# Graph attention layer: the index list copied first in a group, two operands in PSUM, the next scores between the adds

## The reference

```
s_u = x @ W_u.T + b_u                # 8 heads
s_v = x @ W_v.T
e = s_u[src] + s_v[dst]
e = jnp.where(e >= 0, e, 0.2 * e)
m = segment_max(e, dst)
e_exp = jnp.exp(e - m[dst])
denom = segment_sum(e_exp, dst)
msg = xh[src] * (e_exp / denom[dst])[:, None, :]
out = segment_sum(msg, dst)
x = layernorm(x + out)
```

## Time and profile before

| what | value |
|---|---|
| median of 3 runs | 4935.61 us (4934.03 to 4941.12) |
| profiled execution, its own time | 4929.81 us |
| its span | 4928.1 us |
| PE busy | 3099.3 us, 63% |
| VectorE busy | 2202.6 us, 45% |
| GpSimd busy | 3434.9 us, 70% |
| ScalarE busy | 908.4 us, 18% |
| gathers of layer 1 (L1466), 880 | 1008.1 us busy, 605.6 us idle before them |

### The profile page before, as it was taken

The page is one execution under the profiler, slowest core; times in us unless marked ns, Lnnn a source line. Parts: engine busy times, 40 slices in busy tenths (PEclk is TensorE's granted clock), DMA queues, the critical chain, the costliest instruction groups (busy, mean ns, idle before and its releaser), DMA issues. The chain is left out here.

```text
span 4928.1 us, 61408 instructions
## 1 busy us (share of the span) xinstructions
PE 3099.3 (63%) x13554; PEld 1900.6 (39%) x13555; DVE 2202.6 (45%) x5019; ACT 908.4 (18%) x2810; POOL 3434.9 (70%) x2948
## 2 busy tenths in 40 slices
PE   3547877777777777877778768834444444444441
PEld 1224444444444444444444435523333333333331
DVE  2543333333333333333333349855555555555554
ACT  0212222222222222222222223300000000000002
POOL 4238888888888888888888867756666666666564
PEclk9869898888998888888898889956666666666665
DMA  7777767667767677677677666643333333333332
GB/s 285 193 241 137 135 126 136 133 123 135 132 126 138 127 131 134 126 135 132 123 136 132 123 133 206 181 148 93 95 92 100 93 94 91 96 98 94 92 93 66
DMA packets 471760, 641.52 MB, mean 130 GB/s; under 512 B 173608, under 2 KB 365636, under 8 KB 467887
## 3 DMA queue, kind: packets, MB, share of 16 engines
q0 software_dynamic: 198144, 339.26, 36.4%
q1 hardware_dynamic: 245994, 254.83, 17.6%
q10 hardware_dynamic: 27588, 47.08, 3.0%
HBM read 448.23 MB, written 192.71 MB: 130 GB/s over the span
## 5 line engine op out<-in xcount | busy, mean ns | idle before, releaser
L935 POOL DMA_INDIRECT S<-l_msum,l_sink x784 | 1280.7, 1634 | 254.2 <-issue 213.5
L1466 POOL DMA_INDIRECT l_feats<-X_rows,l_gsrc x880 | 1008.1, 1146 | 605.6 <-DVE l_gsrc L1574 340.7
L918 POOL DMA_INDIRECT l_ga<-A_rows,l_gsrc x784 | 791.3, 1009 | 265.6 <-issue 155.4
L1008 PE MATMUL l_psU<-l_hid,l_same 128*128 128x257 f32 x1568 | 585.0, 458 | 534.7 <-ACT l_hid L1044 518.2
L981 PE MATMUL l_psC<-l_table,l_onehot 128*128 x4728 | 726.5, 295 | 0.0
L1532 PE MATMUL l_psU<-l_feats,l_same 128*128 128x264 f32 x1760 | 555.7, 481 | 146.5 <-DVE l_feats L1699 129.2
L1048 ACT COPY l_msum<-l_psU 128x257 f32<-128x257 f32 x784 | 292.6, 373 | 1883.8 <-POOLq L934 1296.1
L974 PE MATMUL l_psC<-W1cT,l_attrT 64*128 64x256 f32 x1576 | 619.0, 476 | 13.1 <-DMA l_table<-B_rows 13.1
L981 PEld LDWEIGHTS l_psC<-l_table,l_onehot 128*128 128x128 bf16 x4728 | 426.0, 104 | 364.9 <-issue 303.4
L1008 PEld LDWEIGHTS l_psU<-l_hid,l_same 128*128 128x128 f32 x1568 | 266.1, 213 | 669.9 <-ACT l_hid L1044 598.9
L1532 PEld LDWEIGHTS l_psU<-l_feats,l_same 128*128 128x128 f32 x1760 | 413.8, 242 | 281.8 <-issue 189.2
(11 more groups left out here) (346 smaller groups left out, 3512.2 us busy)
## 6 DMA issues: line engine op xcount, KB each, us to landing
l_srcb<-src_rows SPq DMA_DIRECT2D x99, 512.0 KB
l_locb<-lo_rows SPq DMA_DIRECT2D x55, 512.0 KB
S<-su_zeros ACTq DMA_DIRECT2D x24, 1156.5 KB
l_locb<-loc_rows SPq DMA_DIRECT2D x99, 256.0 KB
nd_sums<-S SPq DMA_DIRECT2D x196, 128.5 KB, 2.2
l_attr<-in_edge_attr SPq DMA_DIRECT2D x98, 256.0 KB
GH_rows<-l_hidden SPq DMA_DIRECT2D x49, 384.0 KB
nd_hidden<-GH_rows SPq DMA_DIRECT2D x49, 384.0 KB, 3.2
```

What stands on the lines that cost most here:

```text
L918: pool.indirect_dma_start(ga[:, s, :], None, D["A"], bass.IndirectOffsetOnAxis(ap=gsrc[h][:, j % HALF:j % HALF + 1], axis=0)).then_inc(gat ...
L935: pool.indirect_dma_start(D[f"S{j % NTAB}"], bass.IndirectOffsetOnAxis(ap=sink[j // HALF][:, j % HALF:j % HALF + 1], axis=0), msum[:, j % ...
L1008: nc.tensor.matmul(psU[j % 2][:, 0:UW], same[j // HALF][:, j % HALF, :], hid[:, j % RING, :], start=True, stop=True).then_inc(agg_done, 1)
L1466: pool.indirect_dma_start(feats[r][:, t, :], None, D["X1"], bass.IndirectOffsetOnAxis(ap=gsrc[r][:, t:t + 1], axis=0)).then_inc(gathered[r ...
```

## The change

Four things in `layer1_phase`. The index copy for group g + 2 moves from the end of iteration g to its start. A new PSUM bank `psW` holds the weights of a group and the pattern `column`, which is copied there once; `find_edge` reads the pattern and the weight products read the weights from there. ScalarE takes the exponential twice, first into `psW` and then into the rows as before, and TensorE waits for the second with the new semaphore `weights_in_rows`. VectorE takes the scores of g + 1 behind the fourth product, then come adds 4 and 5, the local maxima of g + 1, and adds 6 and 7; TensorE turns the scores of g + 1 behind pair 5.

```diff
--- before.py
+++ after.py
@@ -1388,6 +1388,7 @@
         psE = m.ps("psE", [P, 512])
         psM = m.ps("psM", [P, 512])
         psV = m.ps("psV", [P, 512])
+        psW = m.ps("psW", [P, 512])
         psU = [m.ps(f"psU{q}", [P, 512]) for q in range(4)]
         keys_in, tables_ready, table_split = m.sem("keys_in"), m.sem("tables_ready"), m.sem("table_split")
         loc_in = [m.sem(f"loc_in{r}") for r in range(SETS)]
@@ -1399,12 +1400,14 @@
         ends_ready, ends_turned = m.sem("ends_ready"), m.sem("ends_turned")
         carries_ready, carries_turned, shrink_ready = m.sem("carries_ready"), m.sem("carries_turned"), m.sem("shrink_ready")
         max_ready, max_turned = m.sem("max_ready"), m.sem("max_turned")
-        below_ready, weights_ready = m.sem("below_ready"), m.sem("weights_ready")
+        below_ready, weights_ready, weights_in_rows = m.sem("below_ready"), m.sem("weights_ready"), m.sem("weights_in_rows")
         weighted, agg_done, acc_done = m.sem("weighted"), m.sem("agg_done"), m.sem("acc_done")
         dve_step, pool_waited = m.sem("dve_step"), m.sem("pool_waited")
         block = st.enter_context(nc.Block())
 
         ENDS, CARRY, SHRINK = P, P + 2 * GROUP, P
+        weight = psW[:, 0:GROUP * NH].rearrange("p (t h) -> p t h", h=NH)
+        column = psW[:, P:2 * P]
 
         def groups(engine, body):
 
@@ -1522,6 +1525,7 @@
                 pe.wait_ge(max_ready, g + 1)
                 nc.tensor.transpose(psM[:, 0:P], top[:, :], K["ident"][:, :]).then_inc(max_turned, 1)
                 pe.wait_ge(same_ready, g + 1)
+                pe.wait_ge(weights_in_rows, g + 1)
                 for n in range(PAIRS):
                     if n % 2 == 0:
                         pe.wait_ge(weighted, g * 4 + (n // 2 + 1))
@@ -1532,8 +1536,9 @@
                         i = nc.tensor.matmul(psU[n % 4][:, 0:XW], same[:, t, :], feats[r][:, t, :],
                                              start=(t % PAIR == 0), stop=(t % PAIR == PAIR - 1))
                     i.then_inc(agg_done, 1)
+                    if n == 5 and not last:
+                        turn_scores(g + 1, 1 - r)
                 if not last:
-                    turn_scores(g + 1, 1 - r)
                     gather_ends(g + 1)
 
             groups(pe, body)
@@ -1561,7 +1566,8 @@
                 act.wait_ge(carries_turned, g + 1)
                 nc.scalar.activation(shrink[:, :], psE[:, SHRINK:SHRINK + NH], ACT.Exp).then_inc(shrink_ready, 1)
                 act.wait_ge(below_ready, g + 1)
-                nc.scalar.activation(feats[r][:, :, H:XW], below[:, :, :], ACT.Exp).then_inc(weights_ready, 1)
+                nc.scalar.activation(weight, below[:, :, :], ACT.Exp).then_inc(weights_ready, 1)
+                nc.scalar.activation(feats[r][:, :, H:XW], below[:, :, :], ACT.Exp).then_inc(weights_in_rows, 1)
                 if not isinstance(g, int) or g < XG - SETS:
                     act.wait_ge(sv_done, g + 1)
                     stage_window(g + SETS, r)
@@ -1578,7 +1584,7 @@
                 nc.vector.tensor_scalar(onehot[:, :, :], locb[r][:, :, :], K["winid"][:, 0:1], None, ALU.is_equal).then_inc(onehot_ready, 1)
 
             def find_edge(g):
-                nc.vector.tensor_tensor(same[:, :, :], K["column"][:, :].unsqueeze(1).to_broadcast([P, GROUP, P]),
+                nc.vector.tensor_tensor(same[:, :, :], column.unsqueeze(1).to_broadcast([P, GROUP, P]),
                                         K["loX"][:, bass.ds(g * GROUP, GROUP)].unsqueeze(2).to_broadcast([P, GROUP, P]),
                                         ALU.is_equal).then_inc(same_ready, 1)
 
@@ -1627,6 +1633,7 @@
             split_float(nc, first_steps, K["svf"][:, :, :], svrest[:, :, :],
                         [table[:, :, n * NH:(n + 1) * NH] for n in range(NSPLIT)])
             dve.sem_inc(table_split, 1)
+            nc.vector.tensor_copy(column, K["column"][:, :])
             nc.vector.memset(ones[:, :], 1.0)
             nc.vector.memset(forth[:, 0:1], LOW)
             nc.vector.memset(carry[:, 1, GROUP - 1:GROUP], LOW)
@@ -1653,6 +1660,8 @@
                 c = Chain(dve, dve_step, base)
                 at = bass.ds(g * GROUP, GROUP)
 
+                if not isinstance(g, int) or g < XG - SETS:
+                    stage_index(g + SETS, r)
                 if not last:
                     find_node(g + 1, 1 - r)
                 if not first:
@@ -1693,19 +1702,18 @@
                     c.link(nc.vector.tensor_tensor(rows, rows, factor[:, :].unsqueeze(1).to_broadcast([P, XW // NH, NH]), ALU.mult))
                 dve.wait_ge(weights_ready, g + 1)
                 for q in range(4):
-                    f = feats[r][:, q * QUARTER:(q + 1) * QUARTER, :]
-                    f3 = f[:, :, 0:H].rearrange("p t (c h) -> p t c h", h=NH)
-                    w3 = f[:, :, H:XW].unsqueeze(2).to_broadcast([P, QUARTER, H // NH, NH])
+                    f3 = feats[r][:, q * QUARTER:(q + 1) * QUARTER, 0:H].rearrange("p t (c h) -> p t c h", h=NH)
+                    w3 = weight[:, q * QUARTER:(q + 1) * QUARTER, :].unsqueeze(2).to_broadcast([P, QUARTER, H // NH, NH])
                     nc.vector.tensor_tensor(f3, f3, w3, ALU.mult).then_inc(weighted, 1)
                     if q == 1 or q == 2:
                         add_sums(g, (2 * q - 2, 2 * q - 1), blocks, first)
                 blocks = pair_words(g, 1)
-                add_sums(g, (4, 5, 6, 7), blocks)
                 if not last:
                     take_scores(g + 1, 1 - r, c)
+                add_sums(g, (4, 5), blocks)
+                if not last:
                     local_max(g + 1, 1 - r, c)
-                if not isinstance(g, int) or g < XG - SETS:
-                    stage_index(g + SETS, r)
+                add_sums(g, (6, 7), blocks)
                 if first:
                     steps["first"] = c.n
                 elif "every" not in steps:
```

## The result

The changed kernel took 5080.2 us (median, 5078.0 to 5085.5) where the kernel before took 4938.4 (4934.0 to 4941.6): a ratio of 1.0289, with an interval of 1.0272 to 1.0307. It is 2.9% slower; 6.9% faster was forecast. Timed again twice, it gave two answers: 1.0230 (1.0213 to 1.0247) in one session and 0.9239 (0.9223 to 0.9256) in another. A session is a stretch in which several kernels run on one chip and share the runs of the kernel before.

| kind of session | kernel before, us | changed kernel, us |
|---|---|---|
| late | 4938 (the result), 4931, 4931 | 5080 (the result), 5045 |
| punctual | 4899, 4903, 4909 | 4534 |

The account below looks back on a forecast made before the run. The prediction took GpSimd's gathers and VectorE's index copy waiting for each other, 29.0 us a group, as the bound. 19.3 us plus 53 periods of 22.7 make 1222.4 instead of 1564.4; 340 us saved gives 4595 us, range 4540 to 4700.

Parts of the forecast that it names:

- The ring of the earlier trace: Layer 1: GpSimd and VectorE wait for each other once a group; 3.9 + 23.6 + 1.9 = 29.4 us a period.
- rival (1): Layer 1 gathers: PSUM operands free nothing, GpSimd becomes the bound at 24.2 us a period, 4675 us; chance 0.13.
- PSUM operands set the gathers free: Compare and weight products stop holding GpSimd's gathers: 20.6 us a group instead of about 23.6.
- the 0.6 us put back for the short instructions: Gathers now also run beside scores, scans and one-hot compare, which may hold some: 0.6 us a group, an estimate.
- PSUM costs VectorE nothing: Compare and products with a broadcast PSUM operand take no longer; bounds nothing to one more cycle per element.
- rival (4): The slower side: VectorE reads broadcast PSUM operands slowly, 6.4 us more a group, 4941 us, or 5287; chance 0.05.
- VectorE's chain and the moved scores: VectorE, scores to fourth product: 20.39 us plus 1.94 for adds 4 to 7 in between, 22.3 us a group.
- The 0.3 and 0.1 us: Added to VectorE's 22.3 us: 0.3 for short instructions waiting on gathers, 0.1 for TensorE's clock falling; period 22.7 us.
- (2): TensorE's pairs 6 and 7 fall to the lower clock level, up to 1.8 us a group, 4690 us; chance 0.08.
- (3): TensorE keeps the higher clock for pairs 0 and 1, the chain loses about 2 us, 4495 us; chance 0.06.
- at 20.6 GpSimd is off the chain: With gathers at 20.6 us a group, GpSimd no longer sets the period; VectorE's chain does, 22.7 us.
- GpSimd waiting long for the aggregation: In layer 1, a sign listed beforehand that would show the forecast wrong; no size given.

Follow-up runs that it names:

- e1: Kernel before with only the index copy moved to the head of the iteration: ratio 0.9472 to the kernel before.
- e10: Kernel before with the index copy first and only the compare's pattern in PSUM: ratio 0.9352 to the kernel before.
- e11: Kernel before with the index copy first and only the weights in PSUM: ratio 0.9340 to the kernel before.
- e8: Kernel before with the index copy first and both operands in PSUM, scores not moved: ratio 0.9357 to the kernel before.
- e16: Kernel before with index copy first, both PSUM operands and a GpSimd memset behind each gather: ratio 1.0422 to the kernel before.
- e17: Kernel before with index copy first, both PSUM operands and four GpSimd memsets behind the eighth gather only: ratio 0.9349 to the kernel before.
- e14: Kernel before with the index copy first and the moved scores, no PSUM operands: ratio 0.9550 to the kernel before.
- e15: Kernel before with the index copy first alone, run again unaltered in a later session: ratio 0.9466 to the kernel before.
- e2: Changed kernel with the index copy put back at the end of the iteration: ratio 1.0178 to the kernel before.

## Why the prediction was wrong

The forecast was 4595 us, the range 4540 to 4700; the result was 5080. By its own steps:

- **The ring of the earlier trace rows, and the index copy.** Right: no wait for the copy is left, and alone the copy gives 5.3% (e1). Without PSUM operands it leaves GpSimd as the bound: 16 x (1.18 + 0.30) = 23.7 us of a period of 24.1, near the 24.2 of rival (1).
- **PSUM operands set the gathers free.** Right: 962 ns each with an issue gap of 0.30, 20.2 us a group in the mean against 20.6 forecast and 23.6 in the earlier trace rows, so rival (1) doesn't happen; the 0.6 us put back for the short instructions were 0.2. The rule of the Trainium skill cited for it, in "SBUF — State Buffer", section "Who interferes with whom", that a VectorE instruction with two SBUF inputs contends with a gather's reads and one with a single SBUF input, outside the two-port modes, doesn't, is borne out by both forms: e10 (compare) leaves the long gathers at the products, e11 (weights) those at the compare, e8 none.
- **PSUM costs VectorE nothing.** Right: 1215 ns against 1220 and 2290 against 2282, so rival (4) doesn't happen. The longer fixed latency from PSUM, cited from "VectorE: DVE Perf Modes" of the Trainium skill, section "The TRN2 errata — SBUF-src ops pay a fixed extra latency per instruction", would be 65 ns an instruction by an estimate from its figures; these two rows show 5 ns less and 8 ns more.
- **VectorE's chain and the moved scores.** Right in its parts in the punctual session, where VectorE is never held by the other engines for long. The scan starts at S + 2.38 (forecast 2.45), the one-hot compare at S + 4.80, behind adds 6 and 7 (forecast 4.8). The chain was forecast at 20.39 + 1.94 = 22.33 us and the period is 22.1. The 0.3 and 0.1 us that I had added for meetings with gathers and for the clock weren't there. The saving was put at 340 us; it is 4909.0 - 4534.1 = 374.9. From first to last scores 1222.4 us were forecast and 1190.7 measured, which is 31.7 of the 34.9 us between them. So even there the time, 4534, lies below the range of 4540 to 4700. Neither rival on the clock happens: pairs 6 and 7 run in a stretch of granted clock 1.00 (4007.40 to 4009.40), which was (2), and the first two adds still come 2.00 us apart (4022.05 and 4024.05), at 0.50, which was (3).
- **The step that failed** is "at 20.6 GpSimd is off the chain". It took for granted that GpSimd's gathers cost the others nothing but the ports, and that a product of TensorE is known to its readers as soon as it ends, as the trace of before showed it in each group (0.04 us to the shrink). In the result's trace the period is 31.5 us instead of 22.7, and 1701.9 us pass from the first scores to the last instead of 1222.4: 479.5 of the 485 us by which the forecast missed. The trace of before was of the late kind too; by the account above the kernel before was saved by its own fault. Its wait of 5.9 us for the index copy broke the row of gathers in each group, and so did the gathers of 2.44 and 1.87 us beside the compare and the products. The change took both away, 16 gathers ran into one unbroken row, and the update of the carries, due in the median 12.8 us into it, came 9 us late.
- **The other side.** The rival that was to end slower had the wrong mechanism. "GpSimd waiting long for the aggregation" is what the profile shows; but it is the effect, since the wait that comes first in the ring is VectorE's for the carries.

**What is shown and what isn't.** Shown: the same kernel is 441 (index copy and PSUM operands) and 511 to 546 us (the changed one) apart between the two kinds of session. Of these, 416 and 485 to 511 us lie between the first scores and the last, where the kernel stands in waits for TensorE's semaphores. The other 26 to 37 us lie ahead of layer 1, which begins at 3256 to 3272 us in the late traces and at 3231 to 3242 in the punctual ones; that is about what the kernel before differs by, and why those phases differ is open. Shown too: in the late sessions the kernels with unbroken rows lose and those with broken rows gain; updates at the carries come late in old rows, and come about when the row ends.

Not shown: that a break put in on purpose cures it, since e16 and e17 met a punctual session. That the PSUM operands themselves hold the updates is unlikely: e14 has updates over 4 us late without them, and in the group shown above the compare is done with its PSUM operand at 4034.41, 7 us before the update is used. But no kernel with these operands and a broken row ran in a late session. A rival that no run excludes is the recording: every timed run carries a span and a granted clock, so all were recorded, and it is the late traces that lack records. What makes a session late stays open altogether.

## What to carry to other kernels

When an edit takes the last pause out of a queue of gathers, ask who depended on the pause. Here the kernel measured 8% faster or 3% slower with the same instructions, so time such an edit in more than one session, and look at how long the first reader of a TensorE product waits behind it, not only at the engines' busy shares. In the late sessions the index copy alone is the best kernel run, 4666 to 4669 us (0.947), where the whole change loses 2 to 3%; it was not run in a punctual one. In the punctual ones the whole change is the best, 4534 us (0.924). The index copy with one operand in PSUM keeps some long gathers and was run in punctual sessions only.

## What was unexpected of the hardware

**Late semaphore updates.** In a late session, in the kernels with unbroken rows at the carries, the reader of TensorE's product started 9 to 10 us behind the end of the matmul in the median, after the row of gathers had run on (8.6 us in the lines at 4032.22 and 4041.37), and the two engines that waited for it started at the same instant. The profile gives the kind away even where the time doesn't: in the section on DMA issues the late traces, that of before among them, lack landing times that the punctual ones have. The same kernel, late and then punctual (KB each, us to landing):

```profile
l_srcb<-src_rows SPq DMA_DIRECT2D x99, 512.0 KB
```

```profile
l_srcb<-src_rows SPq DMA_DIRECT2D x99, 512.0 KB, 5.0
```

The landing time of that line is missing on the page of each late trace and is there on each punctual one. The late trace holds 43153 records of semaphore updates, the punctual one of the same kernel 69863.

**VectorE's own counting slows as well.** In the result's trace, the register operations that VectorE's queue runs between instructions, 0.04 to 0.2 us before, took up to 0.8 us, 148 of them over 0.5 us; in the late group shown the drops' product starts at 4031.50, S + 9.8, against 4013.03, S + 7.1, in the punctual one. By the ring above this costs little by itself: the update came near the end of the row, however early the product was ready. In e1, e15 and e2 and in the punctual sessions none took over 0.5 us; in e14 ten did.
